# Third level's attention begun by tiles of the expert layer's result, output stored tile by tile

## The chip, the cores and the metric

The kernel runs on one core of one Trainium2 chip. The metric is device time in microseconds (us) of one execution. Five engines work side by side: TensorE (PE, with its weight loads as PEld), VectorE (DVE), ScalarE (ACT), GpSimd (POOL) and SyncE (SP), which here only issues DMAs. They meet through semaphores.

## The reference, cut to what matters

Four decoder levels, each an attention, a cross attention and a feed-forward layer, with a LayerNorm of the residual sum after each of them. The activations are x of 4 batches x 512 tokens x 512 features. The change touches three of the layers:

```python
# level 2, feed-forward: 64 experts, 8 of them for each token
h = silu(x @ w_gate[e]) * (x @ w_up[e]);  y = sum over the 8 of weight * (h @ w_down[e])
x = _layernorm(x + y)
# level 3, attention (16 heads of 32)
q, k, v = x @ Wq + bq, x @ Wk + bk, x @ Wv + bv
att = softmax(causal(q @ k.T / sqrt(32)))
y = einsum('bhij,bihd->bihd', att, v) @ Wc + bc      # the row sum of att times v
x = _layernorm(x + y)
# level 3, feed-forward, after a cross attention
x = _layernorm(x + gelu(x @ w1_q.T + b1) @ w2_q.T + b2)
```

## The kernel before, in words

x stays in SBUF as `k.X`, 16 tiles of 128 tokens x 512 features (four tiles are a batch). One function per layer writes the instruction stream of every engine. Within a layer, `order()` lists steps, and `tensor()`, `scalar()`, `vector()` and `gpsimd()` each walk that list and issue their engine's part; an engine does its part strictly in that order. `Engine.wait_ge` makes one engine wait for a counted event of another (`"x", n` is tile n of the new x).

**Between layers** `stage()` (L186) is a full barrier: every engine, SP too, waits for all that the engines and all 24 DMA semaphores still have out. Nothing of a layer begins before it, its loads included.

**Expert layer**, `l2_ffn`: 191 blocks of rows gathered by expert. POOL adds the results into two DRAM tables by an indirect DMA with an add (L2824); each add waits for the one two before it in the same table. SP, its queue in program order, loads the weights of the experts, then the four weight matrices of the next attention (`early`, 1 MB each), waits for all adds, and then loads the two tables, four tiles of each at a time (2 x 1 MB, L92 as every DMA). DVE adds them for tile i (L2799) and normalises: `norm(i)` is bn_stats (L247) and bn_aggr (L249) on DVE, two small steps on POOL (L255, L258), and `norm_x(i - 1)` on DVE (L265). So x of tile i - 1 is written after the statistics of tile i.

**Attention**, `l3_attn`: after the barrier, SP loads four biases. PE transposes tiles 0 to 3 (L209), ACT copies them to SBUF (L2544), PE then multiplies the q and k slices m = 0 to 3 of batch 0 (four 128x512 products each, L204), which ACT writes with the bias (L2549). Only then the first scores follow, whose maximum DVE takes (L2583). PE's PSUM banks for this are two (`R`), so the third transpose waits for the first copy.

**Last layer**, `l3_ffn`: for batch b and slice m of 16, "up" is eight products into one of two banks, ACT then makes gelu twice (L3039 in f32, L3041 rounded), DVE the rounding's rest (L3055); "down" is eight products into four banks `YB[t4]`, one bank for each tile of the batch, two slices behind "up". The tile's "finish": POOL adds the bias (L3068), DVE adds the bank (L3060), then `norm`. After the last layer SP waits for DVE and stores four batches of 1 MB.

Of the kernel before, what the change touches and what calls it, by code (L numbers as in the profile page):

```python
# [12 lines left out]
P = 128  # L13
NT = 16
# [3 lines left out]
NB = 191  # L18
NE = 64
NW = 4  # L20
NX = 6
LAYERS = 11
# [100 lines left out]
def quad(ap):  # L123
    return ap.rearrange("p (k n) -> p k n", k=4)


def rows(ap):
    return ap.rearrange("(k p) n -> p k n", p=P)


class K:
# [51 lines left out]
            return Banks(self, [self.bank(first + j)[:, 0, :] for j in range(n)])  # L183
        return Banks(self, [self.bank(first + width * j, width) for j in range(n)])

    def stage(self, label):  # L186

        engines = (self.pe, self.act, self.dve, self.pool)
        for e in engines + (self.sp,):
            for o in engines:  # L190
                if self.stages:
                    e.wait_ge(o)
            for i, sem in enumerate(self.dma.sems):
                n = 16 * ((self.dma.n - i + len(self.dma.sems) - 1) // len(self.dma.sems))
                if e.met.get(sem.name, 0) < n:
                    e.met[sem.name] = n
                    e.queue.wait_ge(sem, n)
        for e in engines + (self.sp,):
            e.begin(label) if e is not self.sp else None
        self.dma.stage = label  # L200
        self.stages.append(label)

# [2245 lines left out]

def l3_attn(k):

    nc, ins, pe, act, dve, pool, sp, dma = k.nc, k.ins, k.pe, k.act, k.dve, k.pool, k.sp, k.dma
    k.stage("l3attn")
    k.off = k.base
    SC = float(32) ** -0.5
    WQ, WK, WV, WO = k.early
    BQ, BK, BV, BO = k.alloc([4]), k.alloc([4]), k.alloc([512]), k.alloc([512])
    XT = [k.alloc([4, 512]) for _ in range(2)]
    QT, KT, V = ([k.alloc([4, 512]) for _ in range(2)] for _ in range(3))
    JK, XB, ON = ([k.alloc([512]) for _ in range(2)] for _ in range(3))
    OT = [k.alloc([4, P]) for _ in range(2)]  # L2460
    SM = k.alloc([2, 5, 16])
# [24 lines left out]
    def loads():  # L2486
        for w, n in ((BQ, "_bq"), (BK, "_bk"), (BV, "_bv"), (BO, "_bo")):
            dma.start(sp, w, ins["L3_attn" + n], "w" + n)

    def tensor():  # L2490
        for what, n in order():
            if what == "xt":
                r = quad(R.take("xt", n, by=((act, "xt", n),)))
                for kk in range(4):
                    t = k.tr(r[:, kk, :], k.X[:, n, kk * P:(kk + 1) * P])
                t.then_inc(*pe.done("xt", n))
            elif what in ("q", "k"):
                b, m = divmod(n, 4)
                r = R.take(what, n, by=((act, what, n),))
                pe.wait_ge(act, "xt", 4 * b + 3)  # L2500
                for kk in range(4):
                    t = k.mm(r, (WQ if what == "q" else WK)[:, kk, m * P:m * P + P], XT[b % 2][:, kk, :], kk == 0, kk == 3)
                t.then_inc(*pe.done(what, n))
            elif what == "v":
                b, t4 = divmod(n, 4)
                r = R.take("v", n, by=((dve, "v", n),))
                for kk in range(4):
                    t = k.mm(r, XT[b % 2][:, kk, t4 * P:t4 * P + P], WV[:, kk, :], kk == 0, kk == 3)
                t.then_inc(*pe.done("v", n))
            elif what == "first":  # L2510
                b, t4, m = n // 16, n // 4 % 4, n % 4
                keys = t4 * P + P
                pe.wait_ge(act, "q", 4 * b + m)
                pe.wait_ge(act, "k", 4 * b + m)
                s = [S.take("s", n, j, by=((act, "e", 4 * n + 2 * j + 1),)) for j in range(2)]
                for g in range(4):
                    k.mm(s[g // 2][:, g % 2, 0:keys], QT[b % 2][heads[g], m, t4 * P:t4 * P + P], KT[b % 2][heads[g], m, 0:keys],
                         True, False)
                for g in range(4):
                    t = k.mm(s[g // 2][:, g % 2, keys - P:keys], k.idb, k.mq, False, True)  # L2520
                    if g % 2:
                        t.then_inc(*pe.done("s", n, g // 2))
            elif what == "back":
                r = quad(R.take("on", n, by=((act, "ot", n),)))
                pe.wait_ge(dve, "on", n)
                for kk in range(4):
                    t = k.tr(r[:, kk, :], ON[n % 2][:, kk * P:kk * P + P])
                t.then_inc(*pe.done("on", n))
            elif what == "out":
                r = R.take("y", n, by=((dve, "z", n),))  # L2530
                pe.wait_ge(act, "ot", n)
                for kk in range(4):
                    t = k.mm(r, OT[n % 2][:, kk, :], WO[:, kk, :], kk == 0, kk == 3)
                t.then_inc(*pe.done("y", n))

    def scalar():
        act.wait_ge(dma, "w_bq")
        act.wait_ge(dma, "w_bk")
        for what, n in order():
            if what == "xt":  # L2540
                b, t4 = divmod(n, 4)
                act.wait_ge(pe, "xt", n)
                act.wait_ge(pe, "v", 4 * b - 5) if b >= 2 else None
                nc.scalar.activation(XT[b % 2][:, :, t4 * P:t4 * P + P], quad(R.of("xt", n)), ACT.Copy).then_inc(*act.done("xt", n))  # L2544
            elif what in ("q", "k"):
                b, m = divmod(n, 4)
# [4 lines left out]
            elif what == "first":  # L2551
                i, m = divmod(n, 4)
# [12 lines left out]
                nc.scalar.activation(OT[n % 2], quad(R.of("on", n)), ACT.Copy).then_inc(*act.done("ot", n))  # L2565

    def vector():
        dve.wait_ge(dma, "w_bv")
        for what, n in order():
            if what == "v":  # L2570
                b, t4 = divmod(n, 4)
# [33 lines left out]
                k.norm(n)  # L2605

    def gpsimd():
        pool.wait_ge(dma, "w_bo")
# [6 lines left out]
    loads()  # L2615
    tensor()
    scalar()
    vector()
# [3 lines left out]
def l2_ffn(k):  # L2622
    nc, ins, pe, act, dve, pool, sp, dma = k.nc, k.ins, k.pe, k.act, k.dve, k.pool, k.sp, k.dma
    k.stage("l2ffn")
    k.off = k.base
    XD, YD, TW, EB = k.mXD, k.mYD, k.mTW, k.mEB
    ER, GB = k.alloc([768]), k.alloc([2, 2 * P])
    TT, TV = k.alloc([NB]), k.alloc([NB])
    GU, DN, DB = k.alloc([NW, 4, 384]), k.alloc([NW, 512]), k.alloc([NW, 512])
# [6 lines left out]
    early = k.W - 8200  # L2636
    assert k.off <= k.W and end <= early
    k.early = [k.view(early + 2048 * j, [4, 512]) for j in range(4)]
    gw = GU.rearrange("p s a b -> p (s a b)")
    YL = [[gw[:, 2048 * j:2048 * j + 2048].rearrange("p (a b) -> p a b", a=4) for j in range(2)],  # L2640
          [DN, DB]]
# [5 lines left out]
    def loads():  # L2647
# [22 lines left out]
                          wd[bass.ds(e, 1), P:192].rearrange("a p n -> p (a n)"), "db", m)  # L2670
        for a, n in zip(k.early, ("_q", "_k", "_v", "_o")):
            dma.start(sp, a, rows(ins["L3_attn" + n]), "early" + n)
        for y in range(2):
            sp.queue.wait_ge(sums_in[y], 16 * ((NB + 1 - y) // 2))
        for j in range(4):
# [292 lines left out]
def l3_ffn(k):  # L2968
# [11 lines left out]
    def order():  # L2980
        for t4 in range(4):
            yield "xt", t4
        for b in range(4):
            for m in range(16):
                yield "up", 16 * b + m
                if m >= 2:
                    yield "down", 16 * b + m - 2
                if m == 8 and b < 3:
                    for t4 in range(4):
                        yield "xt", 4 * b + 4 + t4  # L2990
            yield "down", 16 * b + 14
            yield "down", 16 * b + 15
            for t4 in range(4):
                yield "finish", 4 * b + t4

    def loads():
        dma.start(sp, B1, ins["L3_ffn_b1"], "b1")
        dma.start(sp, B2, ins["L3_ffn_b2"], "b2")

    def tensor():  # L3000
        for what, n in order():
# [14 lines left out]
            elif what == "down":  # L3016
                b, m = divmod(n, 16)
                pe.wait_ge(dve, "hl", n)
                for t4 in range(4):
                    c = slice(t4 * P, t4 * P + P)  # L3020
                    if m == 0:
                        pe.wait_ge(dve, "z", 4 * b - 4 + t4)
                    k.mm(YB[t4], HH[n % 4][:, c], W2[:, m, :], m == 0, False)
                    k.mm(YB[t4], HL[n % 4][:, c], W2[:, m, :], False, m == 15).then_inc(*pe.done("yd", n, t4))

    def scalar():
        act.wait_ge(dma, "b1")
# [150 lines left out]
def program(nc, ins, out, counted, layers):  # L3178
    k = K(nc, ins, out, counted)
    k.start()  # L3180
    for layer in STAGES[:layers]:
        layer(k)
    k.sp.wait_ge(k.dve)
    o = out.rearrange("b (t p) d -> p (b t) d", p=P)
    k.dma.stage = "out"
    for b in range(4):
        k.dma.start(k.sp, o[:, 4 * b:4 * b + 4, :], k.X[:, 4 * b:4 * b + 4, :], "out", b)
    for b in range(4):
        k.sp.wait_ge(k.dma, "out", b)


# [15 lines left out]
```

## Time and profile before

| | us |
|---|---|
| three runs | 5517.39, 5526.94, 5533.07 |
| median | 5526.94 |
| the profiled execution | 5515.92 |
| its span (first to last instruction) | 5514.7 |
| PE busy | 4579.7 (83%) |
| DVE busy | 3057.1 (55%) |
| ACT busy | 1655.2 (30%) |
| POOL busy | 1662.9 (30%) |
| mean granted TensorE clock | 0.897 |

The shares are means over eleven layers with different limits, so they say little about the three places of this change; those are read from stretches of the trace. All times of the rows below are us from the start of the span. A row of a timeline gives start, duration, engine, line, operation and operands, and in square brackets how long the engine was idle before it and who released it. L numbers are lines of the kernel before; lines 204 and 209 are helpers for all products and transposes.

### The profile page before, as it was taken

What the parts mean: (1) busy time and instruction counts of PE and PEld (TensorE: products, weight loads), DVE (VectorE), ACT (ScalarE), POOL (GpSimd) and SP (SyncE); (2) the same over time, 40 slices, a digit from 0 to 9 for tenths busy, and PEclk for the clock granted to TensorE, in tenths of its full rate; (3) what the DMA queues carried; (4) which work ended last, traced back from release to release, by engine and by line L of the source; (5) the groups of instructions that cost most, each with busy time, mean ns of one, the idle gap of its engine ahead of it and who ended that gap; (6) DMA issues with size and microseconds to landing.
All of it is one profiled execution on the core that took longest, in us unless ns stands there. A gap on an engine that the chain in (4) does not pass through costs nothing. (4 is left out here: it accounts for less than half of the span.)

```text
span 5514.7 us, 66051 instructions
## 1 busy us (share of the span) xinstructions
PE 4579.7 (83%) x23144; PEld 2467.7 (45%) x23144; DVE 3057.1 (55%) x5554; ACT 1655.2 (30%) x3282; POOL 1662.9 (30%) x1780
## 2 busy tenths in 40 slices
PE   7996888899978766488899888867999997897687
PEld 5772222344435654255433333334555553343465
DVE  5875777667757555788345556552323333455432
ACT  1113676411112111466222222211121111454332
POOL 1223222001114333255101112355555554111411
PEclk9997999999986556799999999878999998898698
DMA  4320000100000001300001111017999987001000
GB/s 141 95 76 9 2 2 1 73 0 0 0 10 1 0 0 19 126 1 1 29 28 38 53 32 35 24 32 184 241 230 236 217 203 169 20 1 43 2 1 31
DMA packets 156615, 331.85 MB, mean 60 GB/s; under 512 B 26017, under 2 KB 39841, under 8 KB 154722
## 3 DMA queue, kind: packets, MB, share of 16 engines
q1 hardware_dynamic: 109314, 227.07, 13.3%
q0 software_dynamic: 46976, 100.56, 9.4%
q8 instruction: 190, 3.11, 0.2%
q14 instruction: 135, 1.11, 0.1%
HBM read 377.88 MB, written 79.30 MB: 83 GB/s over the span
## 5 line engine op out<-in xcount | busy, mean ns | idle before, releaser
L204 PE MATMUL ps<-arena 128*128 128x512 f32 (+18 forms) x18824 | 4016.8, 453 | 596.4 <-ACT arena L1288 74.2
L204 PEld LDWEIGHTS ps<-arena 128*128 128x128 f32 (+7 forms) x18824 | 1933.6, 169 | 2477.8 <-issue 1302.3
L209 PE MATMUL ps<-arena 128*128 128x128 f32 (+2 forms) x3296 | 436.8, 273 | 286.4 <-DVE arena L265 78.7
L209 PEld LDWEIGHTS ps<-arena 128*128 128x128 f32 (+2 forms) x3296 | 355.0, 141 | 467.8 <-issue 240.3
L255 POOL TENSOR_SCALAR arena<-arena 128x1 f32<-128x1 f32 x192 | 67.6, 352 | 1120.6 <-DVE arena L249 1119.0
L2824 POOL DMA_INDIRECT moe_y<-arena x191 | 305.5, 1600 | 301.7 <-DVE arena L2793 236.1
L866 DVE TENSOR_REDUCE arena<-ps 128x2 f32<-128x1024 f32 x256 | 303.8, 1218 | 86.1 <-PE ps L204 85.4
L2389 DVE TENSOR_REDUCE arena<-ps 128x2 f32<-128x256 f32 (+3 forms) x256 | 198.9, 819 | 260.7 <-PE ps L204 260.7
L2363 ACT ACTIVATE arena<-ps 128x1024 f32<-128x1024 f32 (+3 forms) x256 | 166.2, 701 | 580.2 <-PE ps L204 580.2
L2776 DVE SCALAR_TENSOR_TENSOR arena<-ps,arena 128x128 f32<-128x128 f32 x382 | 103.6, 313 | 410.9 <-ACT arena L2763 409.0
L840 ACT ACTIVATE arena<-ps 128x512 f32<-128x512 f32 x512 | 277.6, 597 | 129.1 <-PE ps L204 126.5
L2431 POOL TENSOR_SCALAR_AFFINE_SELECT arena<-arena 128x512 f32<-128x512 f32 x128 | 82.0, 641 | 704.5 <-ACT arena L2363 704.3
L2763 ACT ACTIVATE arena<-ps 128x192 f32<-128x192 f32 x191 | 63.3, 331 | 690.4 <-PE ps L204 690.4
L204 PE MATMUL ps<-r,r 128*128 128x512 f32 x1024 | 248.4, 405 | 25.4 <-DVE r L3055 24.0
L2793 DVE COPY arena<-ps 128x512 f32<-128x512 f32 x191 | 123.1, 686 | 221.6 <-PE ps L204 221.6
L204 PEld LDWEIGHTS ps<-r,r 128*128 128x128 f32 x1024 | 198.4, 194 | 74.1 <-DVE r L3055 25.3
L2817 POOL DMA_INDIRECT arena<-moe_x,arena x191 | 189.5, 992 | 119.1 <-PE ps L209 79.6
L352 DVE MAX8 arena<-arena 128x8 f32<-128x512 f32 x304 | 211.3, 695 | 10.5
L1657 POOL TENSOR_TENSOR arena<-arena 128x1024 f32<-128x1024 f32 x64 | 164.4, 2589 | 165.1 <-DVE arena L1657 163.8
L350 DVE MATCH_REPLACE8 arena<-arena 128x512 f32<-128x512 f32 x304 | 205.3, 675 | 0.0
L2583 DVE TENSOR_REDUCE arena<-ps 128x2 f32<-128x256 f32 (+3 forms) x128 | 104.9, 820 | 128.5 <-PE ps L204 128.5
L2559 ACT ACTIVATE arena<-ps,arena 128x128 f32<-128x128 f32 (+3 forms) x256 | 131.8, 526 | 127.8 <-DVE arena L2586 127.1
(307 smaller groups left out, 3923.3 us busy)
## 6 DMA issues: line engine op xcount, KB each, us to landing
arena<-in_L_ffn_gu SPq DMA_DIRECT2D x191, 768.0 KB
arena<-in_L_ffn_dn SPq DMA_DIRECT2D x191, 256.0 KB
arena<-in_L_ffn_dn SPq DMA_DIRECT2D x191, 128.0 KB
arena<-in_L_ffn_w SPq DMA_DIRECT2D x64, 256.0 KB
moe_y<-arena SPq DMA_DIRECT2D x34, 256.0 KB
arena<-in_L_ffn_w_gate SPq DMA_DIRECT2D x32, 256.0 KB
arena<-in_L_ffn_w_up SPq DMA_DIRECT2D x32, 256.0 KB
arena<-in_L_ffn_w_down SPq DMA_DIRECT2D x32, 256.0 KB
```

Source lines behind the costliest of these rows:

```text
L204: return self.nc.tensor.matmul(out, lhsT, rhs, start=start, stop=stop, skip_group_check=True)
L209: return self.nc.tensor.transpose(out, in_, ident[0:n, 0:n])
L350: nc.vector.match_replace(k.tw, k.tm8, k.tw if j else s, -3.0e38).then_inc(*(dve.done() if j else dve.done("tfree", n)))
L352: nc.vector.max(k.tm8, k.tw).then_inc(*dve.done())
L840: nc.scalar.activation(PT[v][:, t4].rearrange("p h n -> p (h n)"), S2.of("s2", i, j), ACT.Exp).then_inc(*act.done("p", i, j))
L866: nc.vector.tensor_reduce(MX[:, i % 2, 2 * j:2 * j + 2], S1.of("s1", i, j), AX.X, ALU.max, negate=True).then_inc(*dve.done("mx", i, j))
L1657: return f(o[:, :, 0 if op == ALU.add else 1, :], v[:, :, 0, :], v[:, :, 1, :], op)
L2363: nc.scalar.activation(PT[n % 4][:, 2 * j:2 * j + 2, 0:512 - q0], S.of("s2", n, j)[:, :, 0:512 - q0], ACT.Exp, scale=SC).then_inc(*act.don ...
L2389: nc.vector.tensor_reduce(MX[:, i % 2, 2 * j:2 * j + 2, m], S.of("s1", n, j)[:, :, 0:keys], AX.X, ALU.max, negate=True).then_inc(*dve.done ...
L2559: nc.scalar.activation(JK[g % 2][:, 0:keys], S.of("s", n, g // 2)[:, g % 2, 0:keys], ACT.Exp, bias=SM[:, i % 2, 0, h:h + 1], scale=SC, acc ...
L2817: nc.gpsimd.indirect_dma_start(XG[n % NX], None, XD, bass.IndirectOffsetOnAxis(ap=TT[:, n:n + 1].bitcast(U32), axis=0)).then_inc(rows_in[n ...
L2824: nc.gpsimd.indirect_dma_start(YD[n % 2], bass.IndirectOffsetOnAxis(ap=TT[:, n:n + 1].bitcast(U32), axis=0), YG[n % 4], None, compute_op=A ...
```

## The change

1. `stage(label, soft=True)` for the attention leaves every wait of the barrier out. Single waits stand in for it: PE waits for the last silu of the expert layer and, before each transpose of tile n, for x of tile n; ACT waits for the biases; DVE and POOL wait for x of tile 15; the weight matrices are waited for where they are first used.
2. The buffers are laid out anew, so that batch 0 of the attention (XT, QT, KT, V) lies clear of the places into which the two tables are loaded. Batch 1 lies on those, and ACT waits for the sum of tile 15 before it writes there.
3. The four biases are loaded with the `early` weights, in front of SP's wait for the adds, no longer after the barrier.
4. In the last batch of the last layer "down" of slices 12 to 15 is taken out of the order and done for one tile at a time ("last"), with the tile's "finish" right behind it in the list.
5. Each tile of x is stored when it is ready (16 stores of 256 KB, issued by SP inside the last layer) in place of 4 stores of 1 MB at the end.

```diff
-    def stage(self, label):
+    def stage(self, label, soft=False):
...
-                if self.stages:
+                if self.stages and not soft:
                     e.wait_ge(o)
...
-                if e.met.get(sem.name, 0) < n:
+                if not soft and e.met.get(sem.name, 0) < n:
...
 def l3_attn(k):
...
-    k.stage("l3attn")
+    k.stage("l3attn", soft=True)
...
-    BQ, BK, BV, BO = k.alloc([4]), k.alloc([4]), k.alloc([512]), k.alloc([512])
-    XT = [k.alloc([4, 512]) for _ in range(2)]
-    QT, KT, V = ([k.alloc([4, 512]) for _ in range(2)] for _ in range(3))
+    BQ, BK, BV, BO = k.early_b
+    second = [k.alloc([4, 512]) for _ in range(4)]
+    assert k.off <= k.sums_end
+    k.off = k.sums_end
+    first = [k.alloc([4, 512]) for _ in range(4)]
+    XT, QT, KT, V = (list(two) for two in zip(first, second))
...
     def tensor():
+        pe.wait_ge(act, "silu", NB - 1, stage="l2ffn")
         for what, n in order():
             if what == "xt":
+                pe.wait_ge(dve, "x", n, stage="l2ffn")
...
     def scalar():
-        act.wait_ge(dma, "w_bq")
-        act.wait_ge(dma, "w_bk")
+        act.wait_ge(dma, "early_bq", stage="l2ffn")
+        act.wait_ge(dma, "early_bk", stage="l2ffn")
...
+                act.wait_ge(dve, "z", NT - 1, stage="l2ffn") if b else None
...
     def vector():
-        dve.wait_ge(dma, "w_bv")
+        dve.wait_ge(dma, "early_bv", stage="l2ffn")
+        dve.wait_ge(dve, "x", NT - 1, stage="l2ffn")
...
 def l2_ffn(k):
...
             dma.start(sp, a, rows(ins["L3_attn" + n]), "early" + n)
+        for a, n in zip(k.early_b, ("_bq", "_bk", "_bv", "_bo")):
+            dma.start(sp, a, ins["L3_attn" + n], "early" + n)
         for y in range(2):
             sp.queue.wait_ge(sums_in[y], 16 * ((NB + 1 - y) // 2))
...
 def l3_ffn(k):
...
-                if m >= 2:
+                if m >= 2 and (b < 3 or m < 14):
                     yield "down", 16 * b + m - 2
...
-            yield "down", 16 * b + 14
-            yield "down", 16 * b + 15
+            if b < 3:
+                yield "down", 16 * b + 14
+                yield "down", 16 * b + 15
             for t4 in range(4):
+                if b == 3:
+                    yield "last", t4
                 yield "finish", 4 * b + t4
...
+        out = k.out.rearrange("b (t p) d -> p (b t) d", p=P)
+        for i in range(NT):
+            sp.wait_ge(dve, "x", i)
+            dma.start(sp, out[:, i, :], k.X[:, i, :], "out", i)
+        for i in range(NT):
+            sp.wait_ge(dma, "out", i)
...
+            elif what == "last":
+                for m in range(12, 16):
+                    pe.wait_ge(dve, "hl", 48 + m)
+                    c = slice(n * P, n * P + P)
+                    k.mm(YB[n], HH[m % 4][:, c], W2[:, m, :], False, False)
+                    t = k.mm(YB[n], HL[m % 4][:, c], W2[:, m, :], False, m == 15)
+                t.then_inc(*pe.done("yd", 63, n))
...
-    k.sp.wait_ge(k.dve)
-    o = out.rearrange("b (t p) d -> p (b t) d", p=P)
-    k.dma.stage = "out"
-    for b in range(4):
-        k.dma.start(k.sp, o[:, 4 * b:4 * b + 4, :], k.X[:, 4 * b:4 * b + 4, :], "out", b)
-    for b in range(4):
-        k.sp.wait_ge(k.dma, "out", b)
```

How the order of the instructions moves, at the places of which the prediction speaks. In the rows a bracket names the semaphores that an instruction waits for; a row with x3 stands for three alike.

PE, from the expert layer's last product to the attention's first; before:

```order
L204 MATMUL ps<-arena 128x512 [waits dma17_landed]
L209 MATMUL ps<-arena 128x128 [waits dma4_landed,dma5_landed,dma3_landed,dma18_landed,dma2_landed,dma19_landed,dma1_landed,dma20_landed,dma0_landed,dma21_landed,l2ffn_pool_done,dma22_landed,l2ffn_dve_done,dma23_landed,l2ffn_act_done,l2
L209 MATMUL ps<-arena 128x128 x7
L209 MATMUL ps<-arena 128x128 [waits l3attn_act_done]
L209 MATMUL ps<-arena 128x128 x3
```

and with the change:

```order
L205 MATMUL ps<-arena 128x512 [waits dma17_landed]
L210 MATMUL ps<-arena 128x128 [waits l2ffn_dve_done,l2ffn_act_done]
L210 MATMUL ps<-arena 128x128 x3
L210 MATMUL ps<-arena 128x128 [waits l2ffn_dve_done]
...
L210 MATMUL ps<-arena 128x128 [waits l3attn_act_done,l2ffn_dve_done]
...
L205 MATMUL ps<-arena 128x512 [waits dma18_landed,l3attn_act_done]
```

The instructions are the same and in the same order; the wait for everything has become a wait for one tile of x before each group of four transposes.

PE, the end of the last layer (names ending in 62464 and 62466 are the halves of x, 62467 to 62470 the rounded gelu of four slices, 62471 to 62474 its rest); before:

```order
L204 MATMUL ps<-r4_62464,r1_61577 128x512
L204 MATMUL ps<-r6_62466,r1_61577 128x512
...
L204 MATMUL ps<-r2_61578,r8_62468 128x512
L204 MATMUL ps<-r2_61578,r12_62472 128x512
...
L204 MATMUL ps<-r2_61578,r9_62469 128x512
L204 MATMUL ps<-r2_61578,r13_62473 128x512
...
L204 MATMUL ps<-r2_61578,r10_62470 128x512
L204 MATMUL ps<-r2_61578,r14_62474 128x512
```

and with the change (the numbers of the same buffers are 9 lower):

```order
L205 MATMUL ps<-r4_62455,r1_61568 128x512
L205 MATMUL ps<-r6_62457,r1_61568 128x512
L205 MATMUL ps<-r2_61569,r7_62458 128x512
L205 MATMUL ps<-r2_61569,r11_62462 128x512
L205 MATMUL ps<-r2_61569,r8_62459 128x512
L205 MATMUL ps<-r2_61569,r12_62463 128x512
L205 MATMUL ps<-r2_61569,r9_62460 128x512
L205 MATMUL ps<-r2_61569,r13_62464 128x512
L205 MATMUL ps<-r2_61569,r10_62461 128x512
L205 MATMUL ps<-r2_61569,r14_62465 128x512
```

Before, a slice's eight products (four tiles) stood together, each pair four times over; now the four slices of one tile stand together, and this piece of eight rows comes four times, once for each tile.

SP, around its wait for the adds; before:

```order
L92 DMA arena<-in_L_attn_o 128x4x512 [waits dma21_landed]
L92 DMA arena<-moe_y 128x4x512 [waits dma22_landed,moe_sums1_in,moe_sums0_in]
```

and with the change:

```order
L92 DMA arena<-in_L_attn_o 128x4x512 [waits dma21_landed]
L92 DMA arena<-in_L_attn_bq 128x4 [waits dma22_landed]
L92 DMA arena<-in_L_attn_bk 128x4 [waits dma23_landed]
L92 DMA arena<-in_L_attn_bv 128x512 [waits dma0_landed]
L92 DMA arena<-in_L_attn_bo 128x512 [waits dma1_landed]
L92 DMA arena<-moe_y 128x4x512 [waits dma2_landed,moe_sums1_in,moe_sums0_in]
```

The four biases have moved from behind the barrier to the front of the loads of the two tables (`moe_y`).

## Rows read from the trace of the kernel before

**Rows 1.** Who waited for whom, 4600 to 4745 us: waiter, releaser, total, times, longest

```profile
PE ps L209 <- DVE arena L265: 53.0, 1, 53.0
DVE arena L2583 <- PE ps L204: 35.7, 1, 35.7
```

**Rows 2.** Windows: length, busy us of each engine (instructions), PE clock, DMA share, GB/s

```profile
4675.00:4704.80 29.80, 0.00 (x0) 0.00 (x0) 28.04 (x60) 0.00 (x0) 18.81 (x31) 0.50 0.47 165
4704.90:4713.30 8.40, 6.68 (x20) 4.39 (x21) 0.00 (x0) 2.28 (x4) 1.26 (x1) 0.50 0.21 64
```

**Rows 3.** Timeline, the expert layer's sums and x of tiles 0, 3 and 15

```profile
4672.23 0.69 DVE L2799 TENSOR_TENSOR arena<-arena 128x512 f32<-128x512 f32 x1 [19.56 <-DMA arena<-moe_y]
...
4675.31 0.51 DVE L265 TENSOR_SCALAR arena<-arena 128x512 f32<-128x512 f32 x1
...
4681.24 0.52 DVE L265 TENSOR_SCALAR arena<-arena 128x512 f32<-128x512 f32 x1
...
4704.21 0.55 DVE L265 TENSOR_SCALAR arena<-arena 128x512 f32<-128x512 f32 x1 [0.71 <-POOL arena L258]
```

**Rows 4.** Timeline, from the attention's first instruction to its first maximum

```profile
4704.96 1.94 PE L209 MATMUL ps<-arena 128*128 128x128 f32 x8 [53.03 <-DVE arena L265]
...
4706.24 0.43 SPq L92 DMA_DIRECT2D arena<-in_L_attn_bo  x1
...
4709.59 1.26 POOL L2612 TENSOR_TENSOR arena<-arena 128x512 f32<-128x512 f32 x1 [5.41 <-DMA arena<-in_L_attn_bo]
4709.78 0.60 ACT L2544 ACTIVATE arena<-ps 128x512 f32<-128x512 f32 x1 [0.26 <-PE ps L209]
4710.53 29.86 PE L204 MATMUL ps<-arena 128*128 128x512 f32 x76 [0.78 <-ACT arena L2544]
4715.62 0.69 ACT L2549 ACTIVATE arena<-ps,arena 128x512 f32<-128x512 f32 x1 [5.24 <-PE ps L204]
4719.06 0.69 ACT L2549 ACTIVATE arena<-ps,arena 128x512 f32<-128x512 f32 x1 [2.75 <-PE ps L204]
...
4740.41 0.42 DVE L2583 TENSOR_REDUCE arena<-ps 128x2 f32<-128x256 f32 x1 [35.66 <-PE ps L204]
```

**Rows 5.** Timeline, the last adds into the tables and SP's loads behind them

```profile
4651.18 1.55 POOL L2824 DMA_INDIRECT moe_y<-arena  x1 [6.24 <-DMA moe_y<-arena]
...
4659.33 1.55 POOL L2824 DMA_INDIRECT moe_y<-arena  x1 [4.43 <-DMA moe_y<-arena]
4663.97 2.19 SPq L92 DMA_DIRECT2D arena<-moe_y  x4
```

**Rows 6.** Window (columns as rows 2) in which the four early weight matrices land

```profile
4644.00:4656.00 12.00, 5.58 (x14) 1.74 (x14) 3.08 (x8) 0.00 (x0) 4.04 (x3) 0.97 1.03 324
```

**Rows 7.** Timeline, the last two slices of the last layer and its first tile

```profile
5478.56 0.69 ACT L3039 ACTIVATE arena<-ps,arena 128x512 f32<-128x512 f32 x1 [2.45 <-PE ps L204]
...
5482.27 0.69 ACT L3039 ACTIVATE arena<-ps,arena 128x512 f32<-128x512 f32 x1 [2.45 <-PE ps L204]
...
5483.57 0.69 DVE L3055 TENSOR_TENSOR r<-arena,r 128x512 fp32r<-128x512 f32 x1 [3.03 <-ACT r L3041]
5486.46 0.69 DVE L3060 TENSOR_TENSOR arena<-arena,ps 128x512 f32<-128x512 f32 x1 [2.20 <-PE ps L204]
```

**Rows 8.** Timeline, x of tile 15 and the stores

```profile
5501.47 0.55 DVE L265 TENSOR_SCALAR arena<-arena 128x512 f32<-128x512 f32 x1 [0.71 <-POOL arena L258]
5502.04 3.51 SPq L92 DMA_DIRECT2D out<-arena  x4
```

**Rows 9.** Window (columns as rows 2) of the output stores

```profile
5503.00:5514.00 11.00, 0.00 (x0) 0.00 (x0) 0.00 (x0) 0.00 (x0) 0.00 (x0) 0.50 1.03 379
```

**Rows 10.** Windows (columns as rows 2): after a pause, early and late in the program

```profile
5285.00:5290.00 5.00, 4.68 (x11) 3.72 (x12) 1.76 (x3) 1.27 (x2) 2.00 (x2) 0.50 0.02 3
...
1700.00:1750.00 50.00, 41.78 (x100) 24.08 (x100) 48.67 (x43) 13.35 (x52) 29.99 (x26) 0.50 0.00 0
...
4800.00:4900.00 100.00, 94.56 (x437) 42.41 (x436) 60.56 (x121) 56.17 (x183) 10.89 (x15) 1.00 0.00 1
```

More of the change, by code:

```diff
@@ L194, in stage @@
                 n = 16 * ((self.dma.n - i + len(self.dma.sems) - 1) // len(self.dma.sems))
-                if e.met.get(sem.name, 0) < n:
+                if not soft and e.met.get(sem.name, 0) < n:
                     e.met[sem.name] = n
                     e.queue.wait_ge(sem, n)
-        for e in engines + (self.sp,):
-            e.begin(label) if e is not self.sp else None
+        for e in engines:
+            e.begin(label)
         self.dma.stage = label
@@ L2449, in l3_attn @@
 def l3_attn(k):
[L2451 to L2452 removed]
+    nc, pe, act, dve, pool, dma = k.nc, k.pe, k.act, k.dve, k.pool, k.dma
+    k.stage("l3attn", soft=True)
     k.off = k.base
@@ L2484, in order @@
                     yield what, (t - lag) // 4
-    def loads():
-        for w, n in ((BQ, "_bq"), (BK, "_bk"), (BV, "_bv"), (BO, "_bo")):
-            dma.start(sp, w, ins["L3_attn" + n], "w" + n)
     def tensor():
+        pe.wait_ge(act, "silu", NB - 1, stage="l2ffn")
         for what, n in order():
             if what == "xt":
+                pe.wait_ge(dve, "x", n, stage="l2ffn")
                 r = quad(R.take("xt", n, by=((act, "xt", n),)))
@@ L2500, in tensor @@
                 pe.wait_ge(act, "xt", 4 * b + 3)
+                pe.wait_ge(dma, "early_" + what, stage="l2ffn")
                 for kk in range(4):
@@ L2506, in tensor @@
                 r = R.take("v", n, by=((dve, "v", n),))
+                pe.wait_ge(dma, "early_v", stage="l2ffn")
                 for kk in range(4):
@@ L2531, in tensor @@
                 pe.wait_ge(act, "ot", n)
+                pe.wait_ge(dma, "early_o", stage="l2ffn")
                 for kk in range(4):
@@ L2607, in gpsimd @@
     def gpsimd():
-        pool.wait_ge(dma, "w_bo")
+        pool.wait_ge(dma, "early_bo", stage="l2ffn")
+        pool.wait_ge(dve, "x", NT - 1, stage="l2ffn")
         for what, n in order():
@@ L2613, in gpsimd @@
                 k.norm_rstd(n)
-    loads()
     tensor()
@@ L2626, in l2_ffn @@
     XD, YD, TW, EB = k.mXD, k.mYD, k.mTW, k.mEB
+    GU, DN, DB = k.alloc([NW, 4, 384]), k.alloc([NW, 512]), k.alloc([NW, 512])
+    k.sums_end = k.off
     ER, GB = k.alloc([768]), k.alloc([2, 2 * P])
     TT, TV = k.alloc([NB]), k.alloc([NB])
-    GU, DN, DB = k.alloc([NW, 4, 384]), k.alloc([NW, 512]), k.alloc([NW, 512])
     XG = [k.alloc([512]) for _ in range(NX)]
@@ L2635, in l2_ffn @@
     end = k.off
-    early = k.W - 8200
+    early = k.W - 9240
     assert k.off <= k.W and end <= early
     k.early = [k.view(early + 2048 * j, [4, 512]) for j in range(4)]
+    k.early_b = [k.view(early + o, [n]) for o, n in ((8192, 4), (8200, 4), (8208, 512), (8720, 512))]
     gw = GU.rearrange("p s a b -> p (s a b)")
@@ L3182, in program @@
         layer(k)
-    k.sp.wait_ge(k.dve)
-    o = out.rearrange("b (t p) d -> p (b t) d", p=P)
-    k.dma.stage = "out"
-    for b in range(4):
-        k.dma.start(k.sp, o[:, 4 * b:4 * b + 4, :], k.X[:, 4 * b:4 * b + 4, :], "out", b)
-    for b in range(4):
-        k.sp.wait_ge(k.dma, "out", b)
+    if layers < LAYERS:
+        k.sp.wait_ge(k.dve)
+        k.dma.stage = "out"
+        k.dma.start(k.sp, out.rearrange("b (t p) d -> p (b t) d", p=P), k.X, "out")
+        k.sp.wait_ge(k.dma, "out")
 def kernel(**inputs):
```

## The prediction

> **What bounds the kernel at the three places.** The shares of busy time of the whole program say only that PE leads. I read first who waited for whom around the end of the expert layer. PE waits 53.0 us for one instruction of DVE (L265), and DVE then waits 35.7 us for PE [rows 1]. The two engines take turns: first DVE normalises while PE stands, then PE multiplies while DVE stands. The windows say the same: from 4675.00 to 4704.80 us DVE is busy for 28.04 of 29.80 us and PE for none, at a granted clock of 0.50 [rows 2].
>
> The timeline then gives the instants. The first sum starts at 4672.23, x of tile 0 is written at 4675.31 + 0.51 = 4675.82, x of tile 3 at 4681.24 + 0.52 = 4681.76, x of tile 15 at 4704.21 + 0.55 = 4704.76 [rows 3]. PE begins its transposes at 4704.96, 0.20 us after the last x; the barrier's 24 DMA waits cost no more than that. ACT ends the last of the four copies at 4709.78 + 0.60 = 4710.38, the first product of q starts at 4710.53, and DVE gets its first maximum at 4740.41 [rows 4]. In the last layer I read the last two slices, the four finishes, and the stores. Tile 12 is added at 5486.46 [rows 7], tile 15 is written at 5501.47 + 0.55 = 5502.02, the stores are issued at 5502.04 [rows 8] and the span ends at 5514.7. In those last 12.7 us no engine computes; the DMAs move 379 GB/s for 11.00 us [rows 9].
>
> **The attention begins by tiles (parts 1 and 2 of the change).** PE, ACT and DVE issue what they issued; only waits go. Batch 0 needs tiles 0 to 3. PE's queue reaches the first transpose when the expert layer's products are done, 53.0 us before 4704.96, so the wait for x of tile 3 is the last to end. From 4681.76 I count: 0.20 us until PE reacts (as from 4704.76 to 4704.96); four transposes at half clock, half of the 1.94 us that eight took, 0.97; the copy 0.60; 0.15 until PE starts (4710.38 to 4710.53). Together 1.92, so the products start at 4683.7 instead of 4710.53: **26.8 us earlier**. In this are also the 2 us and more that ACT waited for its biases after the barrier. Behind PE's new waits nothing else is queued. The q and k products take 29.9 us from there and end near 4713.6; DVE is through with x of tile 15 at 4704.76 and POOL before that, its last small step being what released that x [rows 3], so neither delays the first maximum. From there on the attention and all that follows it are simply earlier. Batch 1's copies on ACT wait for the sum of tile 15, long done by then.
>
> What is late next is the clock. Before, the clock was at 0.50 for 8.40 us from PE's first transpose [rows 2], and the first group of q took 4715.62 - 4710.53 = 5.09 us against 4719.06 - 4715.62 = 3.44 us for the next [rows 4]: 1.65 us lost. With the change the transposes come as four short bursts, one each 2 us. The nearest row for dense products straight after a pause is 5285.00 to 5290.00, at 0.50 for the whole 5.00 us with PE busy for 4.68 [rows 10], which would lose 4.68 / 2 = 2.3 us, 0.7 more than before. The other end is a clock already up at the first product, 1.65 us gained. I take **-0.7**, since bursts of 1 us are nearer to a pause than to work. The Trainium skill, "TensorE: Matmul & The Clock Gate", section "HAM oscillation — how this bites in real kernels", says that products in bursts shorter than the waits between them leave the engine cold at each burst; by it the gain of 1.65 would not come, and the sum stays as it is.
>
> **The biases in front of the adds (part 3).** Two of 256 KB and two of 2 KB join the 4 MB that land while the last adds run: the DMA engines are full there, 324 GB/s [rows 6]. The last add is issued at 4659.33 and waits 4.43 us for the one two before it, issued at 4651.18; the loads of the tables follow at 4663.97 [rows 5]. Another 0.52 MB at 324 GB/s is 1.6 us. If the adds are queued behind it the whole chain is 1.6 us later, if they are served beside it, nothing. I take **-0.8**, the middle, because the add issued at 4651.18, in the thick of that traffic, had landed only by 4659.33, 3.3 us after this window. SP's own four issues (0.43 us each, [rows 4]) fall into its wait.
>
> **The last slices tile by tile (part 4).** PE's products are the same 64. One slice, up and down, takes 5482.27 - 5478.56 = 3.71 us [rows 7], so eight products 1.86 and a pair 0.46. With the down of slice 61 behind it, up of slice 63 ends 1.86 us sooner, and its gelu starts near 5480.41 instead of 5482.27. From gelu to the end of the rest is 5483.57 + 0.69 - 5482.27 = 1.99 us, so the last operand is there at 5482.40; meanwhile PE does the other three slices of tile 0 (1.4 us) and stands about 0.8 us. The last pair and 0.2 us of reaction bring the add of tile 12 to 5483.05 instead of 5486.46: **3.4 us**. If up 63 did not come sooner it would be 1.5. The later tiles come from PE each 1.9 us, but DVE and POOL need 5502.02 - 5486.46 = 15.6 us for the four, about 4.1 each with the last normalisation: unchanged, and PE's extra 0.8 us lies under it. What is late next is this chain of DVE and POOL.
>
> **The stores (part 5).** Fifteen of sixteen tiles are stored under other work; nothing else moves on the DMAs in the last layer, and the next tile comes 4.1 us later. Of 4.19 MB there remain 0.26 MB behind x of tile 15: 3.93 MB at 385 GB/s (4.19 MB in the 10.9 us of full traffic inside [rows 9]) is **10.2 us** less, leaving 12.7 - 10.2 = 2.5 us from issue to end. The other bound is the load of a 256 KB bias behind another: 4709.59 - 4706.24 = 3.35 us [rows 4], a gain of 9.3. The Trainium skill, "DMA: Bandwidth & Descriptors", gives a fixed cost of about 2.0 us for a DMA and 436 GB/s, which would be an estimate of 2.6 us for this store; its table of patterns tells to merge many small transfers into a large one, which speaks against this part. The rows decide that only the last store counts.
>
> **The sum.** 26.8 - 0.7 - 0.8 + 3.4 + 10.2 = 38.9 us. The profiled execution took 5515.92 us, with the change 5477.0. It lay 11.0 us below the median of its runs, 5526.94, so for a median I say **5488.0**.
>
> **The rivals.** *The clock stays down through q and k.* The eight groups would run at the speed of 1.2 GHz, 8 x 3.44 = 27.5 us longer, less the 1.65 already paid: 25.9. The gain shrinks to 13.0 and the median to 5513.9. For it speaks that PE's activity before is thinner than before; against it that before, the second q group already ran at full clock, 3.44 us for four products as against 5.09 for the first [rows 4]. The rule on bursts of the page on TensorE would, taken alone, end with the last burst and not reach into the products. 6%.
>
> *The clock stays down for the whole first batch, and the kernel becomes slower.* Its place is PE from 4684 to about 4775 us. There is a stretch of the kind: from 1700 to 1750 us PE is busy for 41.78 of 50 us at 0.50 throughout [rows 10]. The attention in full course is busy for 94.56 of 100 us at 1.00 [rows 10], so 90 us of it hold 85 us of products that would take twice as long: 85 - 38.9 = 46 us slower, a median of 5573. It decides from 39 us of full-clock work done at half clock, and by more than 0.3% from 56 us. Against it: in that early stretch DVE is busy for 48.67 of 50 us and holds PE in pieces, which it does not here. 3%.
>
> *The stores are not hidden.* If SP came to them only after the last x, all 4 MB would still follow. 5488.0 + 10.2 = 5498.2. SP has nothing else queued than two loads, so 5%. That the attention doesn't start by tiles at all is excluded by the order of PE's waits.
>
> **How the numbers follow.** My case has 86%. Its bounds are a gain of 26.8 + 1.65 + 3.4 + 10.2 = 42 us and of 26.8 - 0.7 - 1.6 + 1.5 + 9.3 = 35 us. The runs before lay between 9.6 below and 6.1 above their median, so low is 5526.9 - 42 - 10 = 5475, rounded to 5474, and high, with the case of the stores, 5498.2 + 6 = 5504. A measurement of this kernel tells about 0.3% (16.5 us) from no change. Faster by more: my case and the stores, 0.91. Within: the clock through q and k, 0.06. Slower: 0.03.
>
> **What would show it.** In the profile after, PE's wait for L265's successor falls from 53 us to about 24 in front of tile 0, then four groups of four transposes stand 2 us apart; the first product starts about 27 us ahead of its old place relative to the first sum, and some 8 us after x of tile 0; DVE's wait for its first maximum is about 9 us in place of 35.7. The first q group takes 5 to 6 us. From the last gelu of the last layer to the add of tile 12 there are 2.6 us in place of 4.19. The stores are 16, and from the last x to the end there are 2.5 us. I am wrong if the tables' loads start over 1.6 us later behind the last product, if the granted clock is at 0.50 beyond two groups of q and k, or if the cadence of the last four tiles is no longer 4.1 us.

## The result, and the profile after

| | before | changed |
|---|---|---|
| median, us | 5530.0 (4 runs) | 5481.84 (4 runs) |
| lowest to highest | 5517.39 to 5537.98 | 5478.99 to 5491.67 |
| ratio, 95% interval | | 0.9918 [0.9895, 0.9941] |

The changed kernel is faster, by 45 us if the ratio is taken of 5530.0, with an interval of 33 to 58. A second measurement, the run a1_again below, gave 0.9930 [0.9912, 0.9948], which is 38.6 us of 5515.56. The predicted sum was 38.9 us and the predicted median 5488.0 us, between 5474 and 5504; the median came out at 5481.84. The profiled execution took 5491.67 us, with a span of 5490.4, only 24.3 less than before. That the sum of the terms is nevertheless about right is seen only when the two traces are cut into stretches.

Who waited for whom in the changed kernel, 4600 to 4745 us (its line numbers are 1 to 28 higher):

```profile
PE ps L210 <- DVE arena L266: 26.7, 4, 24.2
...
DVE arena L2590 <- PE ps L205: 17.2, 3, 9.9
```

These rows answer to [rows 1]: the wait of 53.0 us is one of 24.2 with three short ones behind it, and of DVE's 35.7 us there are 9.9 left. The timeline of the changed kernel from the first sum to the second copy of q:

```profile
4682.94 0.69 DVE L2810 TENSOR_TENSOR arena<-arena 128x512 f32<-128x512 f32 x1 [19.70 <-DMA arena<-moe_y]
...
4686.68 1.09 PE L210 MATMUL ps<-arena 128*128 128x128 f32 x4 [24.16 <-DVE arena L266]
...
4691.95 0.52 DVE L266 TENSOR_SCALAR arena<-arena 128x512 f32<-128x512 f32 x1
...
4692.52 1.12 PE L210 MATMUL ps<-arena 128*128 128x128 f32 x4 [0.86 <-DVE arena L266]
...
4694.37 10.90 PE L205 MATMUL ps<-arena 128*128 128x512 f32 x19 [0.73 <-ACT arena L2550]
...
4700.58 0.69 ACT L2555 ACTIVATE arena<-ps,arena 128x512 f32<-128x512 f32 x1 [6.31 <-PE ps L205]
4704.02 0.69 ACT L2555 ACTIVATE arena<-ps,arena 128x512 f32<-128x512 f32 x1 [2.75 <-PE ps L205]
```

From x of tile 3 (4692.47) to the first product are 1.90 us. From the first sum to the first product are 11.43 us, before 4710.53 - 4672.23 = 38.30 [rows 3, 4]. The tail of the changed kernel:

```profile
5469.94 0.69 ACT L3067 ACTIVATE arena<-ps,arena 128x512 f32<-128x512 f32 x1 [0.59 <-PE ps L205]
...
5471.99 6.33 PE L205 MATMUL ps<-r,r 128*128 128x512 f32 x26 [0.69 <-DVE r L3083]
5472.76 0.69 DVE L3088 TENSOR_TENSOR arena<-arena,ps 128x512 f32<-128x512 f32 x1 [0.82 <-PE ps L205]
...
5476.86 0.69 DVE L3088 TENSOR_TENSOR arena<-arena,ps 128x512 f32<-128x512 f32 x1 [2.04 <-POOL arena L3096]
...
5487.79 0.55 DVE L266 TENSOR_SCALAR arena<-arena 128x512 f32<-128x512 f32 x1 [0.71 <-POOL arena L259]
```

The last gelu and the add of tile 12 are 2.82 us apart, in [rows 7] 4.19; PE stands 0.69 us for the last rest. Tiles 13 to 15 wait for POOL, as they did before. From the last x (5488.34) to the end are 2.1 us, in [rows 8] 12.7.

The same stretches of all profiled runs, in us, from the start of one instruction to the start of the next that is named. "Expert" is everything from the program's start to the expert layer's last copy of a result (L2793 before); "adds" runs from there to the first sum; "first max" from the first sum to the attention's first maximum; "attention" from there to its x of tile 15; "layers" from that to the first gelu of the last layer; "slices" from the first gelu to the last but one; "to tile 12" from there to the add of tile 12; "four tiles" from that add to the add of tile 15; "last x" from there to where the last x is written; "end" behind it.

| run | expert | adds | first max | attention | layers | slices | to tile 12 | four tiles | last x | end |
|---|---|---|---|---|---|---|---|---|---|---|
| before | 4652.0 | 20.3 | 68.2 | 320.9 | 149.5 | 267.8 | 7.9 | 12.2 | 3.3 | 12.7 |
| changed | 4662.6 | 20.4 | 42.4 | 325.4 | 149.6 | 267.7 | 4.7 | 12.3 | 3.3 | 2.1 |
| a1_again | 4661.8 | 21.0 | 41.6 | 318.2 | 149.3 | 267.5 | 4.6 | 12.3 | 3.3 | 2.1 |
| a2_front | 4654.2 | 20.9 | 42.6 | 319.4 | 148.9 | 267.8 | 7.9 | 12.2 | 3.3 | 12.6 |
| a3_tail | 4658.3 | 21.7 | 69.7 | 319.5 | 149.2 | 267.6 | 4.7 | 12.3 | 3.3 | 2.1 |
| a4_pool_ahead | 4647.7 | 20.9 | 42.9 | 319.5 | 149.2 | 248.9 | 4.7 | 6.4 | 3.3 | 2.1 |
| b1_stores | 4648.5 | 21.1 | 70.0 | 321.7 | 149.6 | 267.7 | 7.9 | 12.2 | 3.3 | 2.1 |
| b2_barrier | 4651.4 | 21.7 | 65.8 | 319.1 | 149.7 | 267.5 | 4.7 | 12.3 | 3.3 | 2.1 |
| b3_more_early | 4648.2 | 24.1 | 41.3 | 318.1 | 149.0 | 267.7 | 4.7 | 12.3 | 3.3 | 2.1 |
| b4_pe_filler | 4653.9 | 22.2 | 39.5 | 320.7 | 149.7 | 267.1 | 4.6 | 12.3 | 3.3 | 2.1 |
| c0_pool_ahead | 4655.5 | 21.7 | 42.4 | 322.0 | 149.7 | 248.8 | 4.7 | 6.4 | 3.3 | 2.1 |
| c1_ahead_filler | 4655.1 | 21.1 | 39.5 | 320.7 | 149.0 | 247.6 | 4.7 | 6.4 | 3.3 | 2.1 |
| c2_rest_between | 4657.8 | 21.9 | 39.5 | 320.6 | 149.0 | 236.6 | 4.7 | 6.4 | 3.3 | 2.1 |

In the first column the runs differ only in buffer addresses and in whether the four biases are already being loaded at its end, and it spreads over 15 us, the attention over 7. It does so for one and the same kernel too: a4_pool_ahead and c0_pool_ahead have the same code, and their first column is 4647.7 and 4655.5. That is where the 24.3 us of the two first profiles come from: 25.8 + 3.2 + 10.6 gained where the change is, 10.6 lost ahead of it and 4.6 in the attention. The changed places of the last layer repeat to 0.1 us, and "first max" to 1.6 us (41.3 to 42.9 in the six runs with the changed front and nothing added to PE).

### The profile page after: what moved, and what is told of

Same layout as the page of the kernel before. It is cut to its first block and busy times, and to the rows that moved or that the text cites. A ratio compares the mean times of both kernels' runs of the same rounds, so it can differ in the third digit from the quotient of the medians.

```text
span 5490.4 us, 66067 instructions
## 1 busy us (share of the span) xinstructions
PE 4589.7 (84%) x23144; PEld 2476.0 (45%) x23144; DVE 3055.3 (56%) x5554; ACT 1654.3 (30%) x3282; POOL 1662.8 (30%) x1780
## 5 line engine op out<-in xcount | busy, mean ns | idle before, releaser
L205 PE MATMUL ps<-r,r 128*128 128x512 f32 x1024 | 248.6, 406 | 25.9 <-DVE r L3083 24.5
```

Of the source, the lines that this page charges most:

```text
L205: return self.nc.tensor.matmul(out, lhsT, rhs, start=start, stop=stop, skip_group_check=True)
```

## The experiments

### a1_again: the changed kernel once more

The attention was 4.6 us longer in the changed kernel's profile, with the same code but other addresses.

> The changed kernel once more. In the first profile of it the stretch from the attention's first maximum (L2590) to the x of its tile 15 took 325.4 us against 320.9 before, although its code is the same. Theory A (the granted clock dips at other instants from run to run): this stretch takes another length this time, between 320 and 326 us, and where it is longer than before the clock rows of the same instants show 0.50. Theory B (the new places of the buffers, or the earlier start, make the attention itself slower): 325.4 us again to within 0.3 us, with clock 1.00 where it is longer. Time against before: 39 us less by the sum (ratio 0.9930); 35 us less if B holds.

Measured: ratio 0.9930 [0.9912, 0.9948], the attention 318.2 us. Theory B is refuted: 7.2 us less from the same kernel. Theory A had the right cause, but its range, 320 to 326 us, was too narrow. In the trace of the changed kernel the clock stands at 0.50 for 34.1 us of the attention, in this one for 20.5 (a mean clock of 0.95 and 0.97). At half clock 13.6 us more lose 6.8 us of work, nearly all of the 7.2. The windows of one such place in the two profiles of the changed kernel, 17 to 27 us behind the first maximum (length, busy times by engine, clock, DMA share, GB/s), first the one with 325.4 us, then this one:

```profile
4742.00:4752.00 10.00, 7.98 (x36) 3.64 (x35) 4.26 (x11) 5.41 (x23) 0.00 (x0) 0.83 0.00 0
```

```profile
4741.00:4751.00 10.00, 7.98 (x46) 3.45 (x44) 4.51 (x12) 5.35 (x23) 0.00 (x0) 1.00 0.00 0
```

PE is busy for as long, but at a mean clock of 0.83 the trace counts 36 products, at 1.00 46.

### a2_front and a3_tail: the two halves

a2_front is the changed kernel with the old `order()` of the last layer and the old stores; of its edit against the changed kernel, in part:

```diff
-                if m >= 2 and (b < 3 or m < 14):
+                if m >= 2:
                     yield "down", 16 * b + m - 2
...
-            sp.wait_ge(dve, "x", i)
-            dma.start(sp, out[:, i, :], k.X[:, i, :], "out", i)
```

> Parts 1 to 3 alone, with the old order of the last slices and the old stores. My theory of independent terms: first product of q 26.8 us earlier against the first sum, clock ramp 1 us worse, together 25 to 26 us less than before, and the last 12.7 us and the 4.19 us from the last gelu to the add of tile 12 are as before. Rival (the gain is given back downstream, since an earlier attention meets something else): under 20 us.

Measured: 0.9955 [0.9941, 0.9968], 24.8 us less, 18 to 33. The first maximum comes 42.6 us behind the first sum, 25.6 less than before, and the last layer takes what it took before.

a3_tail is the kernel before with parts 4 and 5.

> Parts 4 and 5 alone on the kernel before. Theory: 13.8 us less (3.2 for the last slices, 10.6 for the stores), the front as before: 53 us of wait of PE for L265's last x. Rival (stores under the last layer slow its engines down): less than 10 us, with the 64 slices taking longer than 3.71 us each.

Measured: 0.9969 [0.9960, 0.9979], 17.1 us less, 12 to 22; in the trace 3.2 + 10.6 = 13.8, and the slices take 267.6 us as before. In one session the halves sum to 41.9 us and the whole gave 38.6, so no disturbance of one by the other is seen; with intervals of 5 to 10 us to either side, only the stretches say it closely.

### b1_stores: the stores alone

The four runs whose names begin with b were executed once each: 5505.33, 5498.78, 5471.94 and 5476.61 us, in this order, against 5516.99 of the kernel before. One execution is too little for a difference of a few us, so they are read by their stretches.

> Part 5 alone. From the last x to the end 2.1 us in place of 12.7; from the last gelu to the add of tile 12 4.19 us as before. If the small stores cost more than they hide, the last layer's batches take over 72.5 us each.

Measured: 2.1 us behind the last x, 7.9 from the last but one gelu to tile 12, slices 267.7. Part 5 is worth 10.6 us and nothing is paid for it; the other 3.2 us of the tail are part 4. For the same sixteen stores the DMA list of a4_pool_ahead (below) gives KB and the median us to landing:

```profile
out<-arena SPq DMA_DIRECT2D x16, 256.0 KB, 2.0
```

### b2_barrier: the barrier back, the biases still early

```diff
-    k.stage("l3attn", soft=True)
+    k.stage("l3attn")
```

> The changed kernel with the full barrier back ahead of the attention, the biases still loaded early. Theory: the first product starts 3.5 to 5.8 us after x of tile 15 (5.8 before; the wait of ACT for its biases, 2 us, is gone), and 23 to 24 us of the 26.9 are lost. Rival (the early biases carry most of it): under 10 us lost.

Measured: the first product 37.3 us behind the first sum, 4.8 behind x of tile 15 (5.8 before), the first maximum after 65.8 us. At the first product, which comes after 11.4 us in the changed kernel, 25.9 us are lost. At the first maximum it is 22.9 to 24.5 us against the six runs without barrier and filler (41.3 to 42.9). It is less there because this run had the clock at 1.00 from the first product on:

```profile
4710.40:4714.10 3.70, 3.68 (x9) 1.79 (x10) 0.00 (x0) 0.00 (x0) 0.00 (x0) 1.00 0.00 0
```

Its first group of q took 3.71 us to the first copy, where the three runs with the old front took 5.10 to 6.65. Loading the biases early by itself is worth 1 to 2 us at the first product (38.3, 38.3 and 39.3 us behind the first sum in those three). The waits by tiles carry the front.

### b3_more_early: 2 MB more in front of the wait for the adds

The run adds two loads of 1 MB that nobody reads.

```diff
+        for j, n in enumerate(("_v", "_o")):
+            dma.start(sp, k.view(34000 + 2048 * j, [4, 512]), rows(ins["L3_attn" + n]), "extra", j)
```

> The changed kernel with 2 MB more loaded behind the early biases, in front of SP's wait for the adds (a doubled cost; the extra 2 MB are used by nobody). If the adds queue behind the early loads, the 2 MB at 324 GB/s put SP's first table load 6 us later against the last expert product (12.8 us in the changed kernel). If they are served beside them, less than 1.5 us. The 0.5 MB of biases moved it by 0.2 us, against the 0.8 that I took, so I expect about 0.2 to 1.5.

Measured: 24.1 us from the last copy to the first sum, 20.3 to 22.2 in all others, the old kernel's three among them (20.3, 21.7, 21.1). So the 0.5 MB of biases cost nothing that shows, and 2 MB cost 2 to 4 us, less than the 6 of a queue and more than I expected. POOL's adds in this run, with SP's first table load at 4663.11:

```profile
4647.44 1.55 POOL L2837 DMA_INDIRECT moe_y<-arena  x1 [6.26 <-DMA moe_y<-arena]
4649.49 1.55 POOL L2837 DMA_INDIRECT moe_y<-arena  x1 [0.51 <-issue]
4655.55 1.55 POOL L2837 DMA_INDIRECT moe_y<-arena  x1 [4.50 <-DMA moe_y<-arena]
```

The last add is issued 8.1 us after the one at 4647.44 for which it waits, as in [rows 5] (4651.18 to 4659.33). Only the last add is slower: 7.6 us from its issue to SP's load, in [rows 5] 4.6. Behind its issue the DMA engines still move 362 GB/s here:

```profile
4655.50:4660.00 4.50, 0.00 (x0) 0.00 (x0) 0.00 (x0) 0.00 (x0) 1.55 (x1) 0.50 1.07 362
```

in the kernel before 133, and in the changed kernel, whose last add is issued at 4669.66, 231:

```profile
4659.30:4664.00 4.70, 0.00 (x0) 0.00 (x0) 0.00 (x0) 0.00 (x0) 1.55 (x1) 0.50 0.74 133
```

```profile
4669.60:4674.40 4.80, 0.00 (x0) 0.00 (x0) 0.00 (x0) 0.00 (x0) 1.55 (x1) 0.50 0.96 231
```

Between the issue of the last add and SP's first table load the traces show 0.24 MB of loads on SP's queue in the kernel before, 0.70 MB in the changed kernel and 2.19 MB here, in 4.64, 4.82 and 7.56 us. So the biases do reach past the last add. Yet this stretch is 4.6 to 5.0 us long in all twelve other traces, with the biases loaded early or late. The adds are thus served beside the loads: half a megabyte more beside the last one costs nothing that shows, two megabytes cost 2.5 us and more. Where between the two the cost begins, one profile of the larger load does not tell.

### b4_pe_filler: products that nobody reads ahead of the transposes

The run also makes PE wait for the expert layer's last copy and for the matrix of q, which the added products read.

```diff
     def tensor():
         pe.wait_ge(act, "silu", NB - 1, stage="l2ffn")
+        pe.wait_ge(dve, "y", NB - 1, stage="l2ffn")
+        pe.wait_ge(dma, "early_q", stage="l2ffn")
...
+                if n < 4:
+                    for j in range(26 if n == 0 else 1):
+                        k.mm(k.bank(0)[:, 0, :], WQ[:, 0, 0:P], WQ[:, 1, :], True, True)
                 pe.wait_ge(dve, "x", n, stage="l2ffn")
```

> The changed kernel with products that nobody reads on PE: 26 of 128x512 ahead of the first transpose and one ahead of each of the next three. Theory: they keep the granted clock at 1.00 until the first q product, so the first group of q takes 3.44 us in place of 6.2 and the transposes go at full clock; first product 0.5 us earlier, maximum 3.3 us earlier against the first sum, if the filler doesn't itself hold up the transposes. Rival: the filler's last products run at half clock and push the transposes later, no gain or a loss up to 3 us.

Measured: the first product 11.0 us behind the first sum (11.4 without), the first maximum 39.5 us, 1.8 to 3.4 less than the six runs without. The four transposes take 0.60 to 0.66 us, and the window over them has the clock at 1.00:

```profile
4680.00:4687.00 7.00, 5.08 (x23) 2.36 (x21) 6.72 (x15) 2.39 (x4) 4.46 (x7) 1.00 0.56 171
```

The same window of the changed kernel (4686.00 to 4694.00) has 0.50. So with PE idle for 24 us ahead of them, the four groups of transposes do not bring the clock up, and the price is about 2.7 us at the first maximum. The section "HAM oscillation — how this bites in real kernels" of the Trainium skill's "TensorE: Matmul & The Clock Gate" tells of bursts of products that are shorter than the waits between them and find the clock down each time. The low clock agrees, but the lengths do not: in the changed kernel the groups take 1.1 us and the waits between them 0.8 to 0.9. Whether the attention pays for the filler later isn't settled: it took 320.6 to 320.7 us in the three runs with it and 318.1 to 325.4 in the six without.

### a4_pool_ahead and c0_pool_ahead: POOL one tile ahead

In the kernel before and in the changed one, an end of a batch costs 12.2 us for four tiles. At the end of the program this is open time, and three times before it PE waits 8 us for it. POOL adds the bias of a tile behind the small steps of the tile before, and DVE waits for it.

```diff
             if what == "finish":
-                pool.wait_ge(dve, "z", n - 3)
-                nc.gpsimd.tensor_tensor(YS[n % 3], k.X[:, n, :], B2, ALU.add).then_inc(*pool.done("xb", n))
+                for i in ([0, 1] if n == 0 else [n + 1] if n < 15 else []):
+                    pool.wait_ge(dve, "z", i - 3)
+                    nc.gpsimd.tensor_tensor(YS[i % 3], k.X[:, i, :], B2, ALU.add).then_inc(*pool.done("xb", i))
                 k.norm_rstd(n)
```

> The changed kernel with one more edit: in the last layer POOL adds the bias of tile n + 1 ahead of the two small steps of tile n. Theory: the chain of the last four tiles is DVE, POOL's two steps, POOL's bias add (1.26 us), DVE again, 4.07 us a tile; with the bias add out of it DVE's own work bounds, 2.1 to 2.4 us a tile, so about 5 us less at the end, and as much at the three earlier ends of a batch, where PE waits 8 us for DVE: 15 to 22 us less than the changed kernel. Rival (PE's wait at the end of a batch is for something else than the finishes): 5 us less, all of it after the add of tile 12.

Measured: 0.9895 [0.9881, 0.9910], 57.9 us less than before and 19.3 less than the changed kernel in the same session. The four tiles take 6.4 us, the slices 18.8 less. Who waits in the changed kernel's last layer (5260 to 5490 us), then in this one (5235 to 5445):

```profile
PE ps L205 <- DVE r L3083: 24.5, 4, 8.0
DVE arena L3088 <- POOL arena L3096: 24.5, 12, 2.3
```

```profile
PE ps L205 <- DVE r L3083: 7.8, 4, 2.5
DVE arena L3088 <- PE ps L205: 7.4, 4, 2.2
```

DVE's twelve waits for POOL are gone, and PE's three of 8 us are of 2.2 to 2.5. In the trace it is 18.8 + 5.9 = 24.7 us, above the 15 to 22 expected, since 6.3 us for each inner end and not 5 come back; the two medians differ by less, 19.3 us, with intervals of 8 to 10 us to either side of each.

> The kernel with POOL ahead alone again, as the base for the two above: last layer from its first gelu to the last but one 248.9 us, last four tiles 6.4 us from first to last add, ratio to before 0.9895 as last time. The attention from its first maximum to its last x between 318 and 326 us, as the clock falls.

Measured: 0.9884 [0.9868, 0.9901], slices 248.8, four tiles 6.4, attention 322.0: as expected, and the expected ratio of 0.9895 lies inside the interval.

### c1_ahead_filler and c2_rest_between: further

> The changed kernel with both edits that helped: POOL's bias add one tile ahead in the last layer, and the products that nobody reads ahead of the attention's transposes. If the two are independent: 39 + 20 to 25 + 2.7 = 62 to 66 us less than before (ratio 0.988), with the maximum 39.5 us after the first sum and the last layer as in the run with POOL ahead. If the filler raises the chance of dips of the clock later, less.

Measured: 0.9872 [0.9852, 0.9893], 70.8 us less than before, against 64.1 for c0_pool_ahead in the same session. In the trace both gains are there, 39.5 us to the first maximum and 6.4 for the four tiles, so the two add up.

c2_rest_between is c1_ahead_filler with one step of DVE put elsewhere:

```diff
+    def dve_order():
+        steps = list(order())
+        for b in range(3):
+            steps.remove(("up", 16 * b + 16))
+            steps.insert(steps.index(("finish", 4 * b + 2)), ("up", 16 * b + 16))
+        return steps
```

> The run above and one more edit: at the three inner ends of a batch of the last layer DVE computes the rest (L3083) of the next batch's first slice between the finishes of tiles 1 and 2, not behind tile 3. Theory: PE, which there waits 2.2 to 2.5 us for that rest, goes on earlier, up to 2.8 us for each of the three, 5 to 8 us in all. Rival: PE then waits for the banks of tiles 2 and 3, whose finishes are 0.7 us later, and the gain is under 3 us.

Measured: **5441.58 us, 0.9851 [0.9829, 0.9874], 82.4 us less than before**, the fastest kernel of this study. The slices take 236.6 us, 11.0 less than in c1_ahead_filler, more than the 5 to 8 expected. PE no longer stops at the inner ends, and the clock doesn't fall there: three waits of 2.2 to 2.5 us are gone, and PE is busy for 3.9 us less with the same products. The window over the slices in c1_ahead_filler, then in this run:

```profile
5185.30:5432.90 247.60, 237.56 (x1026) 190.84 (x1025) 75.84 (x121) 85.43 (x136) 26.07 (x36) 0.98 0.03 12
```

```profile
5188.70:5425.30 236.60, 233.67 (x1026) 188.83 (x1025) 74.50 (x121) 85.31 (x136) 27.31 (x36) 1.00 0.04 13
```

## Why the prediction was right, point by point

**The attention by tiles, 26.8 us:** right. The first product came 26.87 us nearer to the first sum; from x of tile 3 to it I had 1.92 us and there are 1.90. That these agree so closely is partly luck: PE reacted in 0.05 us and not 0.20, and the last four transposes took 1.15 us to ACT's copy and not 0.97. b2_barrier shows the cause: with the barrier back, 25.9 of the 26.9 us are gone.

**The clock, -0.7 us:** the term can't be told from nothing. The mechanism is there (0.50 until after the first products of q; b4_pe_filler shows what it costs), but before it was the same: from the first product to the first copy of q the three runs with the old front took 5.10, 6.65 and 5.88 us, those with the new 6.21, 5.39, 6.42, 6.68, 6.21 and 5.09. The means are 5.9 and 6.0. b2_barrier, which has the old order too, took 3.71. The step that failed is to take the one value of [rows 4] for a fixed price; the instant at which the clock rises differs from run to run, by up to 3 us with the barrier and 1.6 without.

**The biases in front of the adds, -0.8 us:** not measurable: from the last add to SP's first table load are 4.82 us, before 4.64. The middle between queued and served beside was the wrong estimate, since the adds are served beside the loads. [rows 6] is also headed as the window in which the four early matrices land, but the trace has 0.24 MB of them left behind the issue of the last add; with the biases it is 0.70 MB (b3_more_early). And SP's own issues were not 0.43 us each: the first took 5.42, which still fell into SP's wait.

**The last slices, 3.4 us:** 3.2. PE stood 0.69 us where I said 0.8, and the reaction to the last pair was 0.2 us longer in all than said.

**The stores, 10.2 us:** 10.6. I left 2.5 us for one store and it took 2.1. The prediction's other two figures for it, 2.6 and 3.35 us, were further off; behind the 3.35 there was another load ahead in the queue.

**The sum and the reference:** 38.9 against 45 (33 to 58) and 38.6 (29 to 49). With intervals 20 us wide, that one of them lies within 0.3 of the sum is luck. The terms as measured, 27.1 (first max 69.3 in the mean of three runs with the old front, 42.2 in the mean of the six with the new one), 3.2 and 10.6, make 40.9. The 2.0 us more than the sum are the two subtracted terms, 1.5 us together, of which nothing shows, and some tenths on the others. The two first profiles alone would have said 24.3.

**The rivals:** the clock didn't stay down through q and k (0.50 to 4699.5, then 1.00, in the windows of the changed kernel below), nor for the first batch, of which the first 79 us had a mean clock of 0.96, and the stores were hidden. What I had not priced as a case is that the attention itself varies by 7 us with the clock (a1_again).

```profile
4694.40:4699.50 5.10, 5.10 (x6) 2.13 (x7) 4.93 (x11) 0.00 (x0) 3.50 (x6) 0.51 0.55 201
4699.50:4704.00 4.50, 4.50 (x12) 2.09 (x11) 4.33 (x11) 0.69 (x1) 2.54 (x5) 1.00 1.04 399
```

## What to carry to other kernels

Where two engines take turns at a layer's border, find the last datum that the next layer's first work really needs; what lies between it and the barrier is the gain, and here it came out within 0.1 us of what the timeline said. Compare traces by stretches between events that both have, since two spans of this program differ by 15 us in code that is the same. And look behind the obvious wait: PE's 8 us for DVE was POOL's order of two small steps and one large one, worth 19.3 us, half as much as the whole change.

## What the runs showed of the hardware

The granted clock falls to 0.50 at other instants of the same program in each execution, also in the attention, where PE is busy for 90% of the time. Of the attention the clock stood at 0.50 for 20.5 to 34.1 us, and its length largely went with it, from 318.1 to 325.4 us. In the changed kernel the issue of a 2 KB load behind four of 1 MB held SP's queue for 5.42 us (5.62 in a1_again, 6.16 in a2_front), where such an issue took 0.36 us after the barrier:

```profile
4654.81 5.42 SPq L92 DMA_DIRECT2D arena<-in_L_attn_bq  x1
```

Nothing waited for it here, since SP had only the wait for the adds behind it.
